# Conditional MLP on one core: TensorE's loop at a fixed slot, seven short warm-ups, first weights rounded in halves, and EPS added on GpSimd

## The chip, the cores and the metric

The kernel runs on 1 core of one Trainium2 chip. The metric is the device time of one execution in microseconds (us), the median over several runs.

## What is computed

Sixteen sequences of 512 tokens with 512 features go through one of three small MLPs. Which one is known only at run time, from an integer for each sequence:

```python
out_nr  = gelu(x @ w1_nr  + b1_nr)  @ w2_nr  + b2_nr
out_tsr = gelu(x @ w1_tsr + b1_tsr) @ w2_tsr + b2_tsr
h       = gelu(x @ w1_sr  + b1_sr)            # 512 -> 1024
out_sr  = gelu(h @ w2_sr + b2_sr) @ w3_sr + b3_sr
y = x + where(c == 0, out_nr, where(c == 1, out_tsr, out_sr))
return (y - mean(y)) * rsqrt(var(y) + 1e-5) * gamma + beta
```

All inputs are float32. The drawn conditions are 0 2 0 0 0 0 0 1 2 2 1 2 0 2 2 1: seven sequences of kind NR (0), three of TSR (1), six of SR (2).

## The kernel before

**Products.** Every float32 factor is split into a part rounded to TensorE's fp32r form (`_hi`) and the rest (`_lo`), and each product of 128x128 by 128x512 is three matmuls: hi·hi, hi·lo, lo·hi (`product`, lines 243 to 246; `part`, line 278, for the first layer of NR). A matmul is a weight load and a matmul instruction. An NR or TSR sequence takes 96 matmuls, an SR sequence 240: 10 x 96 + 6 x 240 = 2400.

**Engines.** One sequence is one batch of the loop. TensorE makes the products in PSUM. ScalarE rounds x to `x_hi`, applies the gelu twice (L415 to `g_hi`, L416 back to the bank) and later scales y by `rstd` (L437). VectorE makes `g_lo` (L467) and `x_lo` (L472), adds the residual (L482), takes statistics (L487, L491), adds EPS to the variance (`variance`, L499), and subtracts the mean (`centre`, L494). GpSimd adds the last bias to the residual rows (L616), takes the power -0.5 (`deviations`, L620), adds beta (L628), and in the first two batches splits the SR and TSR weights into hi and lo (L590, L595, L606). SyncE issues the transfers. Semaphores order all of it; each engine works off its own program strictly in order.

**Order around the change.** ScalarE finishes the four tiles of one batch before it starts the gelus of the next. So the first gelus of batch 1 come after the last `rstd` of batch 0, and with them the first `g_lo` that TensorE needs 48 matmuls into batch 1. GpSimd's program in batch 0 (NR) is: bias of tiles 0 and 1, a half of an SR weight pair, bias of tiles 2 and 3, `deviations(0, 2)`, `split_hi` of the pair sr2 0, `deviations(2, 2)`, `split_lo` of that pair, then the pairs sr1 2, sr1 3, sr2 1 and so on. TensorE needs sr1 3 72 matmuls into batch 1, after its first two hidden products of layer 2.

**The start.** TensorE begins with matmuls on a constant: 9 with 512 columns and then 14 with 128 columns (`N_WARM`, `N_WARM_SHORT`), while x and the first weights are loaded and split. For the first two chunks of `w_hi` VectorE does the rounding itself (L570), and TensorE waits for each on `s_first_w` before its first use.

**Control flow.** TensorE's loop over the 16 batches is written by hand (`kinds`): tests for NR, SR, TSR; each body starts with a branch prefetch hint (L388) for the branch at its end (L390), then the loop's own compare and branch (L406) leads back. The other engines' branches have no hints.

Of the kernel before, what the change touches and what calls it, by code (L numbers as in the profile page):

```python
# [6 lines left out]
NBATCH = 16  # L7
T = 512
H = 512
HC = H // P  # L10
TT = T // P
EPS = 1e-5
# [25 lines left out]
FINISHED_BY_OTHERS_END = TT - 1  # L38

N_WARM, N_WARM_SHORT = 9, 14

def conditional_mlp(nc, x, x_t, cond, weights, bias_cols, rows, out):
    fp32, fp32r, i32 = mybir.dt.float32, mybir.dt.float32r, mybir.dt.int32
    ALU, ACT = mybir.AluOpType, mybir.ActivationFunctionType
    ctx = ExitStack()
    with ctx:  # L48
        def sb(name, shape, dt=fp32):
            return ctx.enter_context(nc.sbuf_tensor(name, shape, dt))  # L50

        def sem(name):
            return ctx.enter_context(nc.semaphore(name))
# [4 lines left out]
        w_raw = nc.alloc_sbuf_tensor_at("w_raw", [P, N_WCHUNK, H], fp32, offset=w_place)  # L58
        w_lo = nc.alloc_sbuf_tensor_at("w_lo", [P, N_WCHUNK, H], fp32r, offset=w_place)
        w_hi = sb("w_hi", [P, N_WCHUNK, H], fp32r)  # L60
# [10 lines left out]
        mv = sb("mv", [P, TT, 2])  # L71
        var_eps = sb("var_eps", [P, TT])
# [27 lines left out]
        s_first, s_first_w, s_nr = sem("s_first"), sem("s_first_w"), sem("s_nr")  # L100
# [3 lines left out]
        s_y, s_acc = sem("s_y"), sem("s_acc")  # L104
        s_row = [sem(f"s_x_row{t}") for t in range(TT)]
        s_xb, s_ev, s_bn, s_mv = sem("s_xb"), sem("s_ev"), sem("s_bn"), sem("s_mv")
        s_var = sem("s_var")
        s_own = sem("s_own")
        s_rstd, s_rstd_end = sem("s_rstd"), sem("s_rstd_end")
        s_v, s_v_end = sem("s_v"), sem("s_v_end")  # L110
# [4 lines left out]
        def take(eng, s, n=1):  # L115
            eng.wait_ge(s, n)
            eng.sem_inc(s, -n)  # L117
# [124 lines left out]
        def _(eng):  # L242
# [18 lines left out]
            def last_layer(w, order, claim):  # L261
                seen = 0
                for j, t in order:
                    if j == seen:
                        take(eng, s_gs)
                        seen += 1
                    if claim and j == 0:
                        take(eng, s_acc)
                    n = bass.ts(t, P)
                    sums = product(bank[4 + t][:, :], g_hi[:, j, n], g_lo[:, j, n], w_hi[:, w + j, :], w_lo[:, w + j, :],  # L270
                                   j == 0, j == HC - 1)
                    if j == HC - 1:
                        sums.then_inc(s_y, 1)

            def x_taken(f):

                eng.sem_inc(s_stage[f], 1)

            def part(j, c, which):

                dst, n, w = bank[j][:, :], bass.ts(j, P), W1[NR] + c
                a, b = (w_lo if which == 2 else w_hi), (x_lo if which == 1 else x_hi)
                return eng.matmul(dst, a[:, w, n], b[:, c, :], start=c == 0 and which == 0, stop=c == HC - 1 and which == 2)

            def step(kind, read_next):
                if kind == NR:
                    take(eng, s_x01, 1)
                    for c in range(2):
                        eng.wait_ge(s_first, c + 1)
                        eng.wait_ge(s_first_w, c + 1)  # L290
                        for which in range(3):
                            if which == 1:
                                if c == 0:
                                    eng.wait_ge(s_nr, 1)
                                else:
                                    take(eng, s_x01, 1)
                                    x_taken(0)
                            if which == 2:
                                eng.wait_ge(s_nr, 2 + c)
                            for j in range(HC):  # L300
                                part(j, c, which)
                        if c == 0:
                            read_next()
                    take(eng, s_x23, 1)
                    for c in (2, 3):
                        if c == 3:
                            take(eng, s_x23, 1)
                            x_taken(1)
                        eng.wait_ge(s_first, 3 + c)
                        if c == 2:  # L310
                            eng.wait_ge(s_nr, 4)
                        for j in range(2):
                            part(j, c, 0)
                            part(j, c, 1)
                        eng.wait_ge(s_nr, 3 + c)
                        for j in range(2):
                            sums = part(j, c, 2)
                            if c == 3:
                                sums.then_inc(s_h, 1)
                    for j in (2, 3):  # L320
                        for c in (2, 3):
                            for which in range(3):
                                sums = part(j, c, which)
                        sums.then_inc(s_h, 1)
                    eng.wait_ge(s_nr, 8)
                    last_layer(W2[kind], ORDER, claim=True)
                    return
                take(eng, s_x01, 2)
                x_taken(0)
                take(eng, s_x23, 2)  # L330
                x_taken(1)
                if kind == NONE:
                    read_next()
                    return
                if kind == TSR:
                    eng.wait_ge(s_split["tsr"], 4)
                    for j in range(HC):
                        layer1(kind, j)
                        if j == 0:
                            read_next()  # L340
                    last_layer(W2[kind], ORDER, claim=True)
                    return
                for j in range(4):
                    if j >= 2:
                        take(eng, s_acc)
                    layer1(kind, j)
                    if j == 0:
                        read_next()
                for first in (0, 2, 4):
                    eng.wait_ge(s_split["sr2"], first // 2 + 1)  # L350
                    for j in (first, first + 1):
                        if j != 1:
                            take(eng, s_gs)
                        for i in range(HC):
                            if j == 0 and i == 2:
                                take(eng, s_gs)
                            layer2_sr(j, i)
                    if first < 4:
                        for j in (first + 4, first + 5):
                            if j < 6:  # L360
                                take(eng, s_acc)
                            eng.wait_ge(s_split["sr1"], 4)
                            layer1(kind, j)
                eng.wait_ge(s_split["sr2"], 4)
                take(eng, s_gs, 2)
                for i in range(HC):
                    layer2_sr(6, i)
                    layer2_sr(7, i).then_inc(s_h, 1)
                eng.wait_ge(s_split["sr3"], 2)
                last_layer(W3[SR], ORDER_SR, claim=False)  # L370
# [32 lines left out]
                body(NONE)  # L403
                nc.switch_bb("tensor_kinds_end")

            with eng.Fori(0, NBATCH) as b:  # L406
                kinds(b)

        @block.scalar
# [54 lines left out]
        def _(eng):  # L464
# [24 lines left out]
            def moments(kind, t):  # L489
                take(eng, s_bn)  # L490
                eng.bn_aggr(mv[:, t, :], bn[:, t, :]).then_inc(s_mv, 1)  # L491
# [5 lines left out]
            def variance(t, n=1):  # L497
                take(eng, s_mv, n)
                eng.tensor_scalar(var_eps[:, t:t + n], mv[:, t:t + n, 1], EPS, None, ALU.add).then_inc(s_var, n)  # L499
# [15 lines left out]
            def body(kind, read_next):  # L515
                read_next()
                hidden(kind)
                split_x(0, s_x01, 2)
                split_x(1, s_x23, 2)
                eng.wait_ge(s_rows, 16)  # L520
                for t in range(0, TT, 2):
                    residual(kind, t)
                    residual(kind, t + 1)
                    stats(kind, t)
                    stats(kind, t + 1)
                    moments(kind, t)
                    moments(kind, t + 1)
                    variance(t, 2)
                    centre(kind, t)
                    centre(kind, t + 1)  # L530

# [35 lines left out]

            for c in range(2):
                eng.wait_ge(s_w_piece[c], 16)
                eng.tensor_copy(w_hi[:, c, :], w_raw[:, c, :]).then_inc(s_first_w, 1)  # L570
                x_low(c, c + 1, (s_nr, s_x01)[c])
                eng.wait_ge(s_first_w, c + 1)
                w_low(c, 0)
            x_low(2, 3, s_nr)
            x_low(3, 4, s_x23)
# [10 lines left out]
        def _(eng):  # L586
# [29 lines left out]
                        eng.tensor_tensor(y[:, t, :], y[:, t, :], row[:, kind, :], ALU.add).then_inc(s_xb, 1)  # L616

            def deviations(t, n):
                take(eng, s_var, n)
                eng.tensor_tensor(rstd[:, t:t + n], var_eps[:, t:t + n], power[:, t:t + n], ALU.pow).then_inc(s_rstd, n)  # L620

            def deviation_end(t, done=s_rstd):
# [149 lines left out]
```

## Time and profile before

| | us |
|---|---|
| three runs | 559.85, 559.77, 558.93 (median 559.77) |
| the profiled execution | 559.41 |
| its span, first to last instruction | 557.7 |
| outside the span | 1.7 |

| engine | busy us | share of the span |
|---|---|---|
| TensorE, matmuls (PE) | 549.6 | 99% |
| TensorE, weight loads (PEld) | 453.4 | 81% |
| VectorE (DVE) | 273.9 | 49% |
| GpSimd (POOL) | 248.3 | 45% |
| ScalarE (ACT) | 213.5 | 38% |

Times in the rows are counted from the start of the span. A matmul's duration of 389 ns is longer than its pace, because consecutive matmuls overlap; the pace is the distance between two starts. A name with a q (DVEq) is an engine's sequencer, which waits, branches and issues.

### The profile page before, as it was taken

How to read it: one execution, taken by the hardware profiler on the slowest of the kernel's cores; microseconds unless marked ns; L12 is line 12 of the kernel's file. 1: busy time of each engine (PE TensorE's matmuls, PEld its weight loads, DVE VectorE, ACT ScalarE, POOL GpSimd, SP SyncE). 2: the span in 40 equal slices, each digit the busy share in tenths (PEclk: the TensorE clock that was granted, in tenths of full speed). 3: DMA queues.
4: the chain of work that ended last, by engine and by line, in shares of the span. 5: the costliest groups of instructions: out<-in, count | busy, mean ns of one | idle time of the engine just before them, and what ended most of it. 6: DMA issues, size and time to landing. Idle time of an engine off the chain costs nothing. (4 is left out here: it accounts for less than half of the span.)

```text
span 557.7 us, 8222 instructions
## 1 busy us (share of the span) xinstructions
PE 549.6 (99%) x2423; PEld 453.4 (81%) x2424; DVE 273.9 (49%) x448; ACT 213.5 (38%) x328; POOL 248.3 (45%) x196
## 2 busy tenths in 40 slices
PE   9999999999999999999999999999999999999994
PEld 6888888888888888888888888888888888888883
DVE  5660176775856956114710569112765105601657
ACT  5451336145244354214421452424255124513351
POOL 0979898765674575300430046600174300430056
PEclk9999999999999999999999999999999999999998
DMA  8876405245344444200320044400244100410032
GB/s 313 339 237 190 152 7 196 100 151 188 109 155 145 156 150 141 84 0 0 138 87 0 1 158 142 150 0 0 75 150 159 66 0 29 154 43 0 0 135 91
DMA packets 26370, 61.28 MB, mean 110 GB/s; under 512 B 3058, under 2 KB 3314, under 8 KB 26226
## 3 DMA queue, kind: packets, MB, share of 16 engines
q1 hardware_dynamic: 26208, 60.97, 31.9%
q8 instruction: 6, 0.10, 0.1%
q10 hardware_dynamic: 146, 0.13, 0.1%
q14 instruction: 10, 0.08, 0.1%
HBM read 44.31 MB, written 16.78 MB: 110 GB/s over the span
## 5 line engine op out<-in xcount | busy, mean ns | idle before, releaser
L467 DVE TENSOR_TENSOR g_lo<-bank,g_hi 128x512 fp32r<-128x512 f32 x112 | 77.5, 692 | 251.0 <-DVEq L117 250.9
L415 ACT ACTIVATE g_hi<-bank,bcol 128x512 fp32r<-128x512 f32 x112 | 77.9, 695 | 165.9 <-ACTq L117 164.7
L620 POOL TENSOR_TENSOR rstd<-var_eps,power 128x2 f32<-128x2 f32 x30 | 21.0, 699 | 239.7 <-POOLq L117 239.7
L616 POOL TENSOR_TENSOR y<-y,row 128x512 f32<-128x512 f32 x64 | 95.7, 1514 | 49.1 <-POOLq L117 48.9
L437 ACT ACTIVATE y<-y,rstd 128x512 f32<-128x512 f32 x63 | 42.3, 717 | 166.3 <-ACTq L117 166.3
L244 PE MATMUL bank<-w_hi,g_hi 128*128 128x512 f32 x256 | 99.6, 389 | 0.0
L245 PE MATMUL bank<-w_lo,g_hi 128*128 128x512 f32 x256 | 99.6, 389 | 0.0
L246 PE MATMUL bank<-w_hi,g_lo 128*128 128x512 f32 x256 | 99.6, 389 | 0.0
L244 PE MATMUL bank<-x_hi,w_hi 128*128 128x512 f32 x240 | 93.4, 389 | 0.0
L245 PE MATMUL bank<-x_lo,w_hi 128*128 128x512 f32 x240 | 93.4, 389 | 0.0
L246 PE MATMUL bank<-x_hi,w_lo 128*128 128x512 f32 x240 | 93.4, 389 | 0.0
L628 POOL TENSOR_TENSOR y<-y,row 128x512 f32<-128x512 f32 x63 | 79.5, 1296 | 0.0
L244 PE MATMUL bank<-g_hi,w_hi 128*128 128x512 f32 x192 | 74.7, 389 | 0.0
L245 PE MATMUL bank<-g_lo,w_hi 128*128 128x512 f32 x192 | 74.7, 389 | 0.0
L246 PE MATMUL bank<-g_hi,w_lo 128*128 128x512 f32 x192 | 74.7, 389 | 0.0
L416 ACT ACTIVATE bank<-bank,bcol 128x512 f32<-128x512 f32 x112 | 74.3, 664 | 0.0
L244 PEld LDWEIGHTS bank<-w_hi,g_hi 128*128 128x128 f32 x256 | 48.1, 188 | 10.0
L245 PEld LDWEIGHTS bank<-w_lo,g_hi 128*128 128x128 f32 x256 | 48.1, 188 | 10.0
L246 PEld LDWEIGHTS bank<-w_hi,g_lo 128*128 128x128 f32 x256 | 48.1, 188 | 9.9
L472 DVE TENSOR_TENSOR x_lo<-stage,x_hi 128x1024 fp32r<-128x1024 f32 x30 | 51.6, 1757 | 4.3 <-DVEq L117 4.3
L245 PEld LDWEIGHTS bank<-x_lo,w_hi 128*128 128x128 f32 x240 | 45.1, 188 | 9.3
L246 PEld LDWEIGHTS bank<-x_hi,w_lo 128*128 128x128 f32 x240 | 45.1, 188 | 9.3
(42 smaller groups left out, 580.2 us busy)
## 6 DMA issues: line engine op xcount, KB each, us to landing
y<-x SPq DMA_DIRECT2D x64, 256.0 KB, 3.6
out<-y SPq DMA_DIRECT2D x63, 256.0 KB, 2.5
stage<-x_t SPq DMA_DIRECT2D x31, 512.0 KB, 3.3
w_raw<-weights SPq DMA_DIRECT2D x17, 512.0 KB, 5.1
row<-rows SPq DMA_DIRECT2D x1, 1280.0 KB, 11.0
stage<-x_t SPq DMA_DIRECT2D x2, 256.0 KB, 3.2
w_raw<-weights SPq DMA_DIRECT2D x2, 256.0 KB, 4.0
out<-y SPq DMA_DIRECT2D x1, 128.0 KB, 1.9
```

The costliest lines, as they stand in the source:

```text
L244: eng.matmul(dst, a_hi, b_hi, start=first, stop=False)
L245: eng.matmul(dst, a_hi, b_lo, start=False, stop=False)
L246: return eng.matmul(dst, a_lo, b_hi, start=False, stop=final)
L415: eng.activation(g_hi[:, slot, :], psum, ACT.Gelu, bias=b)
L416: eng.activation(psum, psum, ACT.Gelu, bias=b).then_inc(s_g, 1)
L437: eng.activation(y[:, t, :], y[:, t, :], ACT.Copy, scale=rstd[:, t:t + 1]).then_inc(s_n, 1)
L467: eng.tensor_tensor(g_lo[:, slot, :], psum, g_hi32[:, slot, :], ALU.subtract).then_inc(s_gs, 1)
L472: eng.tensor_tensor(x_lo[:, c, :], stage[:, f, :, :], x_hi32[:, c, :], ALU.subtract).then_inc(done, n)
L616: eng.tensor_tensor(y[:, t, :], y[:, t, :], row[:, kind, :], ALU.add).then_inc(s_xb, 1)
L620: eng.tensor_tensor(rstd[:, t:t + n], var_eps[:, t:t + n], power[:, t:t + n], ALU.pow).then_inc(s_rstd, n)
L628: eng.tensor_tensor(y[:, t, :], y[:, t, :], row[:, R_BETA, :], ALU.add).then_inc(s_fin, 1)
```

## The change

The first two weight chunks are rounded in halves of 256 columns, each half with its own increment of `s_first_w`, and TensorE waits for a half where it first uses it (output chunks 0 and 2 of `which == 0`). For tiles 0 and 1 of every batch but the last, VectorE no longer adds EPS: it only passes a semaphore on, and GpSimd adds EPS itself before the power. Tiles 2 and 3 stay as they were.

```diff
-N_WARM, N_WARM_SHORT = 9, 14
+N_WARM, N_WARM_SHORT = 9, 7
+
+LOOP_SLOT = 80
...
-        s_var = sem("s_var")
+        s_moments, s_eps, s_var = sem("s_moments"), sem("s_eps"), sem("s_var")
...
                     for c in range(2):
                         eng.wait_ge(s_first, c + 1)
-                        eng.wait_ge(s_first_w, c + 1)
                         for which in range(3):
...
                             for j in range(HC):
+                                if which == 0 and j % 2 == 0:
+                                    eng.wait_ge(s_first_w, 2 * c + j // 2 + 1)
                                 part(j, c, which)
...
-            with eng.Fori(0, NBATCH) as b:
+
+            with nc.Fori(0, NBATCH, engines=[eng.engine], head_slot={eng.engine: LOOP_SLOT}) as b:
                 kinds(b)
...
                     moments(kind, t + 1)
-                    variance(t, 2)
+                    if t == 0:
+                        take(eng, s_mv, 2)
+                        eng.sem_inc(s_moments, 2)
+                    else:
+                        variance(t, 2)
                     centre(kind, t)
...
                 eng.wait_ge(s_w_piece[c], 16)
-                eng.tensor_copy(w_hi[:, c, :], w_raw[:, c, :]).then_inc(s_first_w, 1)
+                for half in (slice(0, H // 2), slice(H // 2, H)):
+                    eng.tensor_copy(w_hi[:, c, half], w_raw[:, c, half]).then_inc(s_first_w, 1)
                 x_low(c, c + 1, (s_nr, s_x01)[c])
-                eng.wait_ge(s_first_w, c + 1)
+                eng.wait_ge(s_first_w, 2 * c + 2)
                 w_low(c, 0)
...
             def deviations(t, n):
-                take(eng, s_var, n)
+
+                if t == 0:
+                    take(eng, s_moments, n)
+                    eng.tensor_scalar(var_eps[:, t:t + n], mv[:, t:t + n, 1], EPS, None, ALU.add).then_inc(s_eps, n)
+                    take(eng, s_eps, n)
+                else:
+                    take(eng, s_var, n)
                 eng.tensor_tensor(rstd[:, t:t + n], var_eps[:, t:t + n], power[:, t:t + n], ALU.pow).then_inc(s_rstd, n)
```

## Rows read from the trace of the kernel before

**Rows 1.** The page: busy time by engine, busy tenths of TensorE, granted clock.
```profile
PE 549.6 (99%) x2423; PEld 453.4 (81%) x2424; DVE 273.9 (49%) x448; ACT 213.5 (38%) x328; POOL 248.3 (45%) x196
...
PEclk9999999999999999999999999999999999999998
```
**Rows 2.** Timeline, TensorE, ends of the stream: start, length, engine, line, tiles, count.
```profile
4.61 1.70 PE L375 MATMUL bank<-const-bfloat16-1.0 128*128 128x128 bf16 x14
6.07 1.24 PE L283 MATMUL bank<-x_hi,w_hi 128*128 128x512 f32 x4
7.15 1.07 PE L283 MATMUL bank<-x_lo,w_hi 128*128 128x512 f32 x4
...
550.01 0.39 PE L246 MATMUL bank<-w_hi,g_lo 128*128 128x512 f32 x1
```
**Rows 3.** Timeline, TensorE's weight loads at the start.
```profile
3.76 0.15 PEld L373 LDWEIGHTS bank<-const-bfloat16-1.0 128*128 128x128 bf16 x1 [0.28 <-issue]
4.18 0.15 PEld L375 LDWEIGHTS bank<-const-bfloat16-1.0 128*128 128x128 bf16 x1 [0.28 <-issue]
...
6.00 0.88 PEld L283 LDWEIGHTS bank<-x_hi,w_hi 128*128 128x128 f32 x4
6.92 0.87 PEld L283 LDWEIGHTS bank<-x_lo,w_hi 128*128 128x128 f32 x4
7.83 0.87 PEld L283 LDWEIGHTS bank<-x_hi,w_lo 128*128 128x128 f32 x4
```
**Rows 4.** Timeline, VectorE and ScalarE at the start.
```profile
3.40 0.62 ACT L444 CAST x_hi<-stage 128x512 fp32r<-128x512 f32 x1 [0.57 <-DMA stage<-x_t]
4.43 0.43 DVE L570 CAST w_hi<-w_raw 128x512 fp32r<-128x512 f32 x1 [3.53 <-DMA w_raw<-weights]
4.78 0.69 DVE L560 TENSOR_TENSOR x_lo<-stage,x_hi 128x512 fp32r<-128x512 f32 x1
5.38 0.68 DVE L560 TENSOR_TENSOR w_lo<-w_raw,w_hi 128x512 fp32r<-128x512 f32 x1
7.05 0.43 DVE L570 CAST w_hi<-w_raw 128x512 fp32r<-128x512 f32 x1 [0.99 <-DMA w_raw<-weights]
```
**Rows 5.** Timeline, VectorE across the end of batch 0.
```profile
27.64 1.14 DVE L499 TENSOR_SCALAR var_eps<-mv 128x2 f32<-128x2 f32 x1
28.70 1.40 DVE L494 SCALAR_TENSOR_TENSOR y<-bank,mv,row 128x512 f32<-128x512 f32 x2
...
32.97 0.17 DVE L499 TENSOR_SCALAR var_eps<-mv 128x2 f32<-128x2 f32 x1
33.05 1.40 DVE L494 SCALAR_TENSOR_TENSOR y<-bank,mv,row 128x512 f32<-128x512 f32 x2
37.65 1.47 DVE L467 TENSOR_TENSOR g_lo<-bank,g_hi 128x512 fp32r<-128x512 f32 x2 [3.20 <-DVEq L117]
```
**Rows 6.** Timeline, GpSimd from the biases of batch 0 to sr1 3.
```profile
26.23 2.53 POOL L616 TENSOR_TENSOR y<-y,row 128x512 f32<-128x512 f32 x2
28.97 0.72 POOL L620 TENSOR_TENSOR rstd<-var_eps,power 128x2 f32<-128x2 f32 x1 [0.21 <-POOLq L117]
29.66 1.06 POOL L590 TENSOR_SCALAR w_hi<-w_raw 128x1024 fp32r<-128x1024 f32 x1
33.33 0.70 POOL L620 TENSOR_TENSOR rstd<-var_eps,power 128x2 f32<-128x2 f32 x1 [2.60 <-POOLq L117]
...
41.20 2.40 POOL L595 TENSOR_TENSOR w_lo<-w_raw,w_hi 128x1024 fp32r<-128x1024 f32 x1 [0.18 <-POOLq L117]
```
**Rows 7.** Timeline, ScalarE from the tiles of batch 0 to batch 1's gelu.
```profile
29.80 1.34 ACT L437 ACTIVATE y<-y,rstd 128x512 f32<-128x512 f32 x2 [8.25 <-ACTq L117]
34.15 1.34 ACT L437 ACTIVATE y<-y,rstd 128x512 f32<-128x512 f32 x2 [3.01 <-ACTq L117]
35.88 0.69 ACT L415 ACTIVATE g_hi<-bank,bcol 128x512 fp32r<-128x512 f32 x1 [0.40 <-ACTq L117]
```
**Rows 8.** Timeline, weight loads of batch 1: its first, g_lo's first, sr1 3's first.
```profile
27.78 0.19 PEld L244 LDWEIGHTS bank<-x_hi,w_hi 128*128 128x128 f32 x1
...
38.66 0.19 PEld L244 LDWEIGHTS bank<-g_hi,w_hi 128*128 128x128 f32 x1
...
44.10 0.19 PEld L244 LDWEIGHTS bank<-x_hi,w_hi 128*128 128x128 f32 x1
```
**Rows 9.** By line: L499 on VectorE and GpSimd's smallest operations.
```profile
L499 DVE TENSOR_SCALAR var_eps<-mv x34: 136/169/1142, 27.6 to 553.1; 128x2 f32<-128x2 f32 x30, 128x1 f32<-128x1 f32 x4
...
0.78 0.10 POOL L645 MEMSET power<- 128x4 f32 x1 [0.29 <-POOLq L766]
```
**Rows 10.** TensorE's sequencer, L406 and the hint L388, whole span and around 25 us.
```profile
L406 PEldq COMPARE_BRANCH  x16: 76/213/252, 24.6 to 546.5; - x16
...
L388 PEldq BRANCH_PREFETCH_HINT  x1: 46/46/46, 25.6 to 25.6; - x1
```
**Rows 11.** The page, DMA queues: packets, MB, share. Queues that carry instructions.
```profile
q8 instruction: 6, 0.10, 0.1%
...
q14 instruction: 10, 0.08, 0.1%
```
**Rows 12.** Timeline, VectorE at the end of the span.
```profile
550.40 0.74 DVE L494 SCALAR_TENSOR_TENSOR y<-bank,mv,row 128x512 f32<-128x512 f32 x1
551.05 0.69 DVE L482 TENSOR_TENSOR bank<-bank,y 128x512 f32<-128x512 f32 x1
...
554.32 0.88 DVE L505 SCALAR_TENSOR_TENSOR y<-y,rstd,row 128x256 f32<-128x256 f32 x2 [0.44 <-DVEq L117]
```

## The prediction

> **What bounds the kernel now.** I read the page first: matmuls are busy 99% of the span, every other engine at most half [rows 1]. Then I looked whether TensorE ever pauses. The first real matmul starts at 6.07 us and the last at 550.01 [rows 2]; between them lie 2399 steps, so the mean pace is (550.01 - 6.07)/2399 = 0.2267 us. The stretch from 7.15 to 7.83 in the weight loads, and those around 38.66 and 44.10, have that same pace [rows 3, 8]: (44.10 - 38.66)/24 = 0.2267, (38.66 - 27.78)/48 = 0.2267. A mean over the whole run that equals the pace of single stretches leaves no room for stalls: all of them together are under about 0.2 us. So the time is a sum of three parts: 6.07 before the stream, 543.9 of stream, and 557.7 - 550.01 = 7.7 of tail; with 1.7 outside the span this is the profiled 559.41. The change removes no matmul of the stream, so it can only move the start, move the tail, or put a stall into a stream that has none.
>
> What sets 6.07? The last short warm-up. x_hi is rounded at 3.40 + 0.62 = 4.02 and w_hi at 4.43 + 0.43 = 4.86 [rows 4], while the 14 short warm-ups start at 4.61 and follow one another up to 6.07 [rows 2]. TensorE's real work is ready 1.1 us before it begins.
>
> **Warm-ups, 14 to 7.** The clock first. The 14 warm-ups of 128 columns fill 4.61 to about 6.1, (6.07 - 4.61)/14 = 0.104 us or slightly more each, and the long ones are 0.42 apart (3.76, 4.18) [rows 2, 3]: 512 columns at 1.2 GHz. The four first real weight loads start at 6.00 to 6.69 and the next four at 6.92, i.e. 0.92 for four against 0.91 (7.83 - 6.92) for the next [rows 3]; the matmuls take 7.15 - 6.07 = 1.08 for four, one at 0.39 and three at 0.23. So the level rises to 2.4 GHz inside the first real matmul, after 5.4 us of unbroken work; the page's clock line, which begins with that rise, shows full clock from there to the end of the stream [rows 1]. Seven warm-ups fewer let the first real matmul start 7 x 0.107 = 0.75 us earlier, at 5.32 (0.107 = 0.427/4, a quarter of the columns). If the clock still rises near 6.2, the 0.9 us from 5.32 to 6.2 run at 0.427 per matmul: 2.1 matmuls done, where before 0.3 to 0.4 were. That is 1.75 matmuls ahead, 1.75 x 0.227 = **0.40 us** gained. The other 0.35 us of the 0.75 are lost to the slow clock. Had the clock risen before the short warm-ups, they would cost about half each, and the gain is again 7 x 0.054 = 0.38.
>
> **What the stream then meets.** TensorE arrives 0.40 earlier everywhere; what doesn't follow it can become late. In the first chunk: x_lo ends at 5.47 and is needed at 6.92 - 0.40, w_lo ends at 6.06 and is needed at 7.83 - 0.40 [rows 3, 4]. The second w_hi is bound by its transfer and ends at 7.48; its first use comes four matmuls after the last row of rows 3 (7.83 + 0.91 = 8.74), less 0.40 = 8.34. All have 0.85 or more.
>
> **Halves.** Two rounding operations of 0.43 become four of about half. No row shows a 256-column rounding; bounds for the addition are 0 and the whole of a smallest VectorE operation, 0.17 [rows 9], once per chunk. I take 0.06. It delays x_lo and w_lo by that, inside covers of 0.85; the first half is ready some 0.2 earlier, but 4.86 is already before 5.32. Price and gain: **0**. It would matter only if the clock rises before the short warm-ups, when the first use comes near 5.0 and the second chunk's near 7.6.
>
> **EPS.** The place to look is the end of batch 0. VectorE's L499 takes 0.17 as a rule but 1.14 at 27.64 [rows 5, 9], and it ends at 28.78, when GpSimd's two bias additions end (26.23 + 2.53 = 28.76) [rows 6]: it sat behind them. The next one takes VectorE only 0.08 (32.97 to 33.05) [rows 5]. What follows hangs on it: `centre` at 28.70, the second L499 at 32.97, GpSimd's power at 33.33 after an idle 2.60, ScalarE's tiles at 34.15, its first gelu of batch 1 at 35.88, g_lo at 37.65 [rows 5 to 7]. g_lo's first half-pair ends at 37.65 + 0.69 = 38.34, and TensorE takes it at 38.66 [rows 8]: 0.32 of cover, of which the handover takes some. Likewise sr1 3: w_lo ends at 41.20 + 2.40 = 43.60, needed at 44.10: 0.50 [rows 6, 8]. Neither follows TensorE's start, since VectorE in this stretch waits for GpSimd's biases, and those for transfers. So an earlier start alone would use up these 0.32, and gain 0.0 to 0.3 instead of 0.40.
>
> With the edit VectorE passes the semaphore at about 27.6 and goes to `centre`, 1.14 - 0.08 = **1.06 us earlier**. The residual of tiles 2 and 3 needs biases that end at 27.5 and 28.76, so it can follow. GpSimd adds EPS from about 28.95: price between 0.10 (its memset) and 0.72 (its power) [rows 6, 9], plus 0.18 for taking its own semaphore (the idle time before L595, rows 6). I take 0.25 + 0.18, since a 2-column addition is nearer to the memset. The power then ends at about 30.1 (29.9 to 30.6), split_hi of 1.06 at 31.2 (at most 31.7), before the second power can start at 33.33 - 1.06 = 32.3. ScalarE's first two tiles start at 30.2 to 30.8 and take 1.34, done by 32.1, before 34.15 - 1.06 = 33.1. So both chains arrive 1.0 earlier, g_lo at about 37.3 and sr1 3 at 42.6, against needs of 38.26 and 43.70. Cover: 1.0 and 1.1. In later batches the first `rstd` comes 0.3 to 0.8 later and `centre` 0.1 earlier; queued behind GpSimd's new operation are only its second power, which waits for VectorE anyway, and the beta additions. The power waited for VectorE by 2.6 us in batch 0, and 33.33 - 28.97 = 4.4 us lie between the two powers. I take 0 for this; above, 0.1.
>
> **The loop's place.** TensorE's loop branch costs its sequencer 0.21 (0.25 at most), and it is at the next body's hint at 25.6 while the weight loads of that body start at 27.78 [rows 8, 10]: 2.2 us ahead. Queue 8 moved 6 packets of instructions in the whole run, 16 KB each [rows 11]; 16 passes over three kinds cannot be refetched with so few, so the loop stays loaded. Where no fetch costs anything, a better place has nothing to give: **0**. Its first entry gains one taken branch, 0.2 us, at about 3 to 4 us, more than 1 us before 5.32. Below zero it cannot go, as no stall is there to be removed.
>
> The Trainium skill, "Runtime: NRT & Kernel Launch", section on instruction fetch mechanics, says that a taken branch whose target lies outside the window that is loaded has to wait for a fetch. VectorE's idle 3.20 before 37.65 [rows 5] is such a case as far as the rows go, TensorE's rows show none; by that rule a worse place would be the second rival below.
>
> **The tail.** No edit touches the last batch. VectorE works without a break from TensorE's last matmuls to 554.32 + 0.88 [rows 12], so the tail moves with the stream: 0.
>
> **Sum.** -0.40 (warm-ups) + 0 + 0 + 0 + 0 = -0.40 against the profiled 559.41: 559.0. The profiled execution is 0.36 under the median of the three runs; the median of all four is 559.6, and I predict **559.2**, which is that less 0.40. Runs differ by 0.9 us already. The Trainium skill ("TensorE: Matmul & The Clock Gate", the HAM clock gate) says that the moment of the rise varies from run to run because its window runs free; this trace has one rise and doesn't show it. If it holds, runs with an early rise were held up before at 38.66 and are freed by the EPS edit, up to about 0.7 more.
>
> **The rivals.**
> 1. The earlier start is given back: something else in batch 0 or 1 that is tied to a transfer is late (g_lo or a weight pair), because VectorE's sequencer spends its 3.20 us whenever it gets there, or more at another place in its code. For it: the cover was 0.32 and VectorE's code grows. Against: 1.06 us come free. Time: 559.6. Chance 0.15.
> 2. Slower: the new place puts a piece of TensorE's loop where its hint doesn't cover it. Price of one miss: VectorE's 3.20 less the lead of 2.2 = 1.0 us; in the first passes over each kind one to three of them, 560.2 to 562.2; if every pass misses, 16 us. It decides if the loop spills into one more block than before. Against it: 6 packets only, and the hints. 561. Chance 0.08.
> 3. Slower: with less work ahead of it the clock rises later. If it took its 5.4 us anew from 5.32, it would rise at 10.7 and cost half of 4.5 us: 561.5. Against: the real matmuls follow without a gap and keep TensorE as busy. Chance 0.04.
> 4. Early rises are common and the freed 38.66 counts: 558.3 to 558.6. Chance 0.12.
>
> Forecast 0.61 (558.8 to 559.5).
>
> **Range and chances.** 558.2 to 560.0 takes in the forecast, rivals 1 and 4, and the spread of the runs. About 0.2%, or 1.1 us, is what a measurement of this kernel can tell from no change. Faster by more than that: part of rival 4, 0.06. Slower: rivals 2 and 3 mostly, 0.09. Within: 0.85.
>
> **What the profile will show.** The first L283 matmul at about 5.3 and the last L246 near 549.6; first four real matmuls over a longer time than 1.08; L494 of batch 0 at 27.6 in place of 28.70, and g_lo near 36.6 in place of 37.65; a GpSimd operation of 0.1 to 0.7 ahead of each first power; still 2400 matmuls at 0.2267. A pause in TensorE's loads near a batch's beginning would prove rival 2, one near 38.3 or 43.7 rival 1.

## The result and the profile after

The changed kernel takes 560.81 us (median of 13 runs, 560.28 to 561.29) against 559.77 for the kernel before (13 runs): ratio 1.0019, 95% interval 1.0012 to 1.0027. It is **1.0 us slower**, where 0.4 us faster was forecast. The profiled execution took 560.53 us, its span is 558.5 against 557.7.

First the page, in the lines that answer to [rows 1] and [rows 11], and TensorE's waits (engine, line, waited for: us, times, longest).

```profile
PE 549.4 (98%) x2416; PEld 452.2 (81%) x2417; DVE 271.9 (49%) x435; ACT 213.5 (38%) x328; POOL 251.8 (45%) x211
...
PEclk9999999999999999999999999999999999999998
...
q8 instruction: 7, 0.11, 0.1%
...
PE bank L246 <- PEq L119: 1.0, 1, 1.0
```

The kernel before has no wait of a real matmul in this view; now there is one, of 1.0 us, and it is put down to TensorE's own sequencer. Queue 8 carries one packet of instructions more. Next the timeline of TensorE, matmuls and then weight loads, which answers to [rows 2] and [rows 8]; bracketed is the idle time ahead of a row.

```profile
4.62 0.93 PE L378 MATMUL bank<-const-bfloat16-1.0 128*128 128x128 bf16 x7
5.33 1.20 PE L285 MATMUL bank<-x_hi,w_hi 128*128 128x512 f32 x4
6.37 1.07 PE L285 MATMUL bank<-x_lo,w_hi 128*128 128x512 f32 x4
7.28 1.07 PE L285 MATMUL bank<-x_hi,w_lo 128*128 128x512 f32 x4
8.26 1.16 PE L285 MATMUL bank<-x_hi,w_hi 128*128 128x512 f32 x4
...
11.15 0.42 PE L285 MATMUL bank<-x_hi,w_hi 128*128 128x512 f32 x1
...
27.34 0.39 PE L248 MATMUL bank<-w_hi,g_lo 128*128 128x512 f32 x1
28.75 0.47 PE L246 MATMUL bank<-x_hi,w_hi 128*128 128x512 f32 x1 [1.02 <-PEq L119]
...
550.87 0.39 PE L248 MATMUL bank<-w_hi,g_lo 128*128 128x512 f32 x1
```
```profile
27.12 0.19 PEld L248 LDWEIGHTS bank<-w_hi,g_lo 128*128 128x128 f32 x1
28.72 0.19 PEld L246 LDWEIGHTS bank<-x_hi,w_hi 128*128 128x128 f32 x1 [1.41 <-issue]
```

Between the last matmul of batch 0 (27.34) and the first of batch 1 (28.75) lie 1.41 us where the pace is 0.227. What the sequencer did there stands in the view of the line of the branch that ends a body (L393 after, L390 before; durations in ns: least, median, most): first after, over the whole span, then before.

```profile
L393 PEldq COMPARE_BRANCH  x16: 184/184/3365, 23.5 to 547.0; - x16
```
```profile
L390 PEldq COMPARE_BRANCH  x16: 184/194/449, 23.9 to 546.2; - x16
```

One of the 16 branches, the first, takes 3365 ns in place of 449. It is the one at the end of the first NR body, which starts at 23.51 and ends at 26.88. The trace has a 16 KB packet of instructions on queue 8 that starts at 24.38, after the branch's start. In the kernel before that packet starts at 21.34, ahead of the branch at 23.94.

The sum of the change, from the starts of matmuls (rows above and [rows 2, 8]):

| stretch | before | after | difference |
|---|---|---|---|
| span's start to first real matmul | 6.07 | 5.33 | -0.74 |
| that one to the 25th (before: 11.68) | 5.61 | 5.82 | +0.21 |
| 25th to batch 1's first (28.00, 28.75) | 16.32 | 17.60 | +1.28 |
| batch 1's first to the last (550.01, 550.87) | 522.01 | 522.12 | +0.11 |
| last matmul's start to the end | 7.7 | 7.7 | 0 |
| sum | 557.7 | 558.5 | +0.86 |

### The profile page after: what moved, and what is told of

Its sections match the earlier page's. It is cut to its first block and busy times, and to the rows that moved or that the text cites. A ratio compares the mean times of both kernels' runs of the same rounds, so it can differ in the third digit from the quotient of the medians.

```text
span 558.5 us, 8241 instructions
## 1 busy us (share of the span) xinstructions
PE 549.4 (98%) x2416; PEld 452.2 (81%) x2417; DVE 271.9 (49%) x435; ACT 213.5 (38%) x328; POOL 251.8 (45%) x211
## 5 line engine op out<-in xcount | busy, mean ns | idle before, releaser
L631 POOL TENSOR_SCALAR var_eps<-mv 128x2 f32<-128x2 f32 x15 | 3.3, 217 | 185.6 <-POOLq L119 185.4
L246 PEld LDWEIGHTS bank<-x_hi,w_hi 128*128 128x128 f32 x240 | 45.0, 188 | 10.7 <-issue 1.4
```

Source lines behind the costliest of these rows:

```text
L246: eng.matmul(dst, a_hi, b_hi, start=first, stop=False)
```

## The experiments

All times are medians; the kernel before, run beside them, took 559.6 to 559.9. The letters of the theories are those of the expectations. The measured branch is the one at the end of the first NR body, the pause is what TensorE loses at the start of batch 1 over its pace. Branch and pause come from one profiled execution of each kernel; whether they repeat in the other executions is not shown.

### Which part costs

**The change with a plain loop.** Edit against the changed kernel:
```diff
-            with nc.Fori(0, NBATCH, engines=[eng.engine], head_slot={eng.engine: LOOP_SLOT}) as b:
+            with eng.Fori(0, NBATCH) as b:
```

> The changed kernel with a plain loop, so that its head lies wherever the 7 fewer warm-ups leave it. Theory A (the fixed place makes the loop branch at the end of the first NR body wait for its code: 3.37 us on TensorE's sequencer against 0.45 before): the branch takes 0.45 or less, no pause near 28.7 us, time 559.0 to 559.5. Theory B (the sequencer, with fewer warm-ups queued, issues its hint at 3.3 in place of 4.4 us, and the hint is lost): the 3.4 us branch and the 1.2 us pause stay, 560.8. Theory C (any place other than the old one has a miss): the branch is long too, 560.8, but then not by the time of the hint.

Measured 560.59, ratio 1.0017 (1.0008 to 1.0027); branch 3726 ns, pause 1.6 us. So A falls: without the slot the branch is as long.

**The slot alone**, put into the kernel before (head_slot 80 in its loop).

> The kernel before with the head of TensorE's loop at slot 80 and nothing else. A: the branch at the end of the first NR body takes 3 us or more, one pause of about 1.2 us near 28 us, time 561.0 against 559.8 of before. B: no pause, 559.8. C: as A, if slot 80 is not where the loop lay before.

560.71, ratio 1.0017 (1.0007 to 1.0026); but the branch took 2291 ns and the pause was only 0.13 us. The profiled execution lost more elsewhere: 0.9 at the third chunk, where ScalarE's w_hi was late, and 0.5 where batch 1 first takes g_lo and the pair sr1 3. The slot costs here, and little of it at the branch.

**The warm-ups alone** (`N_WARM_SHORT` 7).

> The kernel before with 7 short warm-ups, nothing else; the loop's head moves 14 instructions forward. A: no long branch; the start is 0.75 us earlier, but the g_lo that TensorE takes at 38.66 ends at 38.3 whatever TensorE does, so the gain is 0.0 to 0.3 us: 559.5 to 559.8. B: a branch of 3.4 us at the end of the first NR body, pause 1.2 us, 560.6 to 561.

559.47, ratio 0.9995 (0.9985 to 1.0005): no change that can be told. Branch 2349 ns, pause 0.2 us.

**EPS alone** (the hunks of `variance` and `deviations`).

> The kernel before with EPS of tiles 0 and 1 added on GpSimd, nothing else; TensorE's program is that of before. All theories: within 0.3 us of before (559.5 to 559.8); the first g_lo of batch 1 ends about 1 us earlier than 38.34, and TensorE has 1.0 to 1.4 us of cover there in place of 0.32. If the EPS edit is itself the cost, 560.5 or more.

559.33, ratio 0.9991 (0.9981 to 1.0000). Branch 449 ns. VectorE's timeline at the end of batch 0 in this kernel, which answers to [rows 5]:

```profile
28.64 0.41 DVE L491 BATCH_NORM_AGGREGATE mv<-bn 128x2 f32<-128x6 f32 x2
29.30 1.41 DVE L494 SCALAR_TENSOR_TENSOR y<-bank,mv,row 128x512 f32<-128x512 f32 x2 [0.25 <-DVEq L117]
...
33.58 0.17 DVE L499 TENSOR_SCALAR var_eps<-mv 128x2 f32<-128x2 f32 x1
```

From the start of the aggregates to `centre` it is 0.66 us; before, where the aggregates start at 27.09, it was 28.70 - 27.09 = 1.61 [rows 5]. The edit frees 0.95 us there. This execution needed them: its loads landed later than those of [rows 5], and g_lo still ended at 38.58 (37.88 + 0.69), just ahead of the weight load at 38.65 that takes it.

**The halves alone**, in the kernel before:
```diff
-                        eng.wait_ge(s_first_w, c + 1)
...
+                                if which == 0 and j % 2 == 0:
+                                    eng.wait_ge(s_first_w, 2 * c + j // 2 + 1)
...
-                eng.tensor_copy(w_hi[:, c, :], w_raw[:, c, :]).then_inc(s_first_w, 1)
+                for half in (slice(0, H // 2), slice(H // 2, H)):
+                    eng.tensor_copy(w_hi[:, c, half], w_raw[:, c, half]).then_inc(s_first_w, 1)
...
```

> The kernel before with the first weights rounded in halves, nothing else; the loop's place stays. A: branch 0.45 us, 559.7 plus or minus 0.3. Halves as the cause: branch 2 us or more and 560.5 or more.

560.73, ratio 1.0021 (1.0012 to 1.0030); branch 3666 ns, pause 1.6 us. The halves alone bring a loss as large as the change's, without adding an instruction to TensorE's program: its loads only carry other waits.

**Warm-ups and EPS, without halves and slot.**

> 7 warm-ups and the EPS edit, no fixed slot, no halves. If the halves make the difference between the 560.6 of the changed kernel without its slot and the 559.5 of the warm-ups alone: branch about 2.3 us, pause 0.1 to 0.2 us, 559.0 to 559.5. If the EPS edit together with the early start does: branch 3.3 to 3.7 us, 560.5. If it is the chance of the profiled execution (the same place, so the same fetch): branch anywhere between 2.3 and 3.7.

559.31, ratio 0.9993 (0.9984 to 1.0003); branch 2409 ns, pause 0.27. This half of the change does what was forecast, as near as it can be measured: 0.35 us below the kernel before, in an interval that holds zero.

**The same with slot 80.**

> 7 warm-ups, the EPS edit and the fixed slot 80, without the halves: the change but for its third part. If slot and halves each cost what they cost alone (0.98 and 1.07) because each makes the same branch wait, this one still has a long branch of 2.3 to 3.6 us and takes 559.4 to 560.8; with the 2.3 us of the slot alone, pause under 0.3 us at 28 us and 559.5. If the slot alone costs by another way (late loads at the start, an extra fetch), 560.3 or more.

560.46, ratio 1.0013 (1.0004 to 1.0022): the slot costs 1.15 us here (560.46 against 559.31), and with it no halves are needed for a loss. The two costs do not add up. In the changed kernel, where the halves are in, the slot costs 0.2 (560.81 against the 560.59 of the plain loop); and where the slot is in, the halves cost 0.35 (560.81 against 560.46). Leaving out one of them would not have saved the change. Branch 2656 ns, pause 0.55; and TensorE waited 0.7 us for the second w_hi:

```profile
PE bank L285 <- DVE w_hi L577: 0.7, 1, 0.7
PE bank L246 <- PEq L119: 0.3, 1, 0.3
```

### Is it the loop's place?

**Slots 94, 110 and 66** in the changed kernel.

> The changed kernel with its loop head at slot 94 in place of 80. Theory A (the head of the kernel before lies at about slot 94, and 7 fewer warm-ups bring it to about 80; what counts is how far ahead of the branch at the end of the first NR body TensorE enters its next block of instructions, since that is when the code behind the branch is fetched; slot 94 puts the crossing 14 instructions earlier than slot 80): the branch takes 0.45 us, its fetch starts near 21 us and not behind the branch, no pause near 28 us, time 559.0 to 559.4. Theory D (it is the wait in front of the branch, or the moved start, and not the place): branch 2 to 3.7 us, time 560.5 or more.

> The changed kernel with slot 110. A: the block is entered 30 instructions (3.4 us) earlier than with slot 80, branch 0.2 to 0.45 us, no pause near 28 us, 559.0 to 559.4; but the end of the loop spills over one more block boundary, which may cost at another branch, in the first passes. D: as slot 80, 560.5 or more.

> The changed kernel with slot 66. A: the block is entered 14 instructions later than with slot 80, 24 instructions ahead of the branch; the branch takes the whole fetch, 3.3 to 3.8 us, pause 1.2 to 1.6 us at about 28.7, time 560.5 to 561.3. If the place doesn't matter: like slot 94.

560.73 (1.0009 to 1.0027), 560.67 (1.0007 to 1.0026) and, in a single execution, 560.38. Branches 3396, 3604 and 2977 ns. No slot cures it. Slot 110 alone has no packet of instructions at 5 to 6 us (slots 66, 80 and 94 have), which I read so (no run shows where the blocks end): its head still fits into the block of the code ahead of it, the others' are pushed into the next, and the head of the changed kernel's plain loop lies between 94 and 110.

**The old place, kept by 14 semaphore updates** ahead of a plain loop.
```diff
+            for n in range(14):
+                eng.sem_inc(s_fill, 1 if n % 2 == 0 else -1)
             eng.sem_inc(s_acc, 4)
...
```

> The changed kernel without the fixed slot, and with 14 semaphore updates of TensorE's sequencer in the place of the 14 instructions of the 7 warm-ups that went. The loop has the place and its head the time (about 4.2 us) that it has in the kernel before; start, halves and EPS edit are those of the change. Theory A (place): branch at the end of the first NR body 0.45 us, its fetch near 21 us, no pause near 28 us, 559.0 to 559.4. Theory E (halves or the early arrival cause the miss, wherever the loop lies): branch 2.3 to 3.7 us, 560.5 or more.

560.76, ratio 1.0020 (1.0011 to 1.0029); branch 3546 ns. And the same without the halves:

> 7 warm-ups and the EPS edit, no halves, no slot, and 14 semaphore updates of TensorE's sequencer that keep the loop where the kernel before has it. Theory A' (without the halves the place decides between a branch of 0.45 and one of 2.3 us): branch 0.45 us, fetch near 21 us, no pause at 28 us, 558.9 to 559.3, faster than the kernel before and about 0.2 us faster than without the 14 updates. Otherwise as without them: 559.3, branch 2.4 us.

560.30, ratio 1.0013 (1.0004 to 1.0022), branch 3469 ns, pause 1.3. That one fell on the wrong side of every theory: no halves, the old place, the hint at the old time, and a long branch. Without the 14 updates the same kernel took 559.31. So the old place does not bring the short branch back.

**No hints**, in the kernel before.

> The kernel before without its branch hints (and so with one instruction fewer in each body). If the fetch at 21.3 us that serves the branch at the end of the first NR body comes from the hint: this fetch is gone, the branch takes 3 us or more, and TensorE pauses 1.2 us near 28 us: 561. If it comes from going on into the next block: branch 0.45 us as before, no pause there.

A single execution: 561.92; branch 5319 ns, no packet ahead of it, pause 3.0 us. TensorE's weight loads:

```profile
26.90 0.19 PEld L246 LDWEIGHTS bank<-w_hi,g_lo 128*128 128x128 f32 x1
30.19 0.19 PEld L244 LDWEIGHTS bank<-x_hi,w_hi 128*128 128x128 f32 x1 [3.10 <-issue]
```

The hints are most likely what makes the 449 ns, though this edit also takes an instruction out of each body. The changed kernel's 3.4 us lie between the branch before and the one without hints.

### Is it the halves' wait, VectorE, or the moment?

**One more wait, long fulfilled, on the third weight load.**
```diff
+                                if which == 0 and j == 2:
+                                    eng.wait_ge(s_first_w, c + 1)
```

> The kernel before with one thing more: in the first chunk products of NR, TensorE's third weight load of each chunk waits for s_first_w once more, which is long reached. No instruction is added, two weight loads only carry a wait. Theory F (what makes the fetch behind the hint come too late in the version with halves is the wait on TensorE's own weight load): branch 3.3 to 3.7 us, 560.5 to 560.9. Theory G (it is the way VectorE now works, or the timing of the start): branch 0.45 us, 559.7.

559.69, ratio 0.9999 (0.9990 to 1.0009), branch 449 ns. F falls.

**Halves on VectorE, one wait on TensorE** (`s_first_w` at `2 * c + 2`, in the old place).

> The kernel before with w_hi rounded in halves on VectorE, but TensorE waiting once for both halves, in the place of its old wait. F: branch 0.45 us, 559.7 plus or minus 0.3. G: branch 2 us or more, 560.5 or more.

559.80, ratio 1.0002 (0.9993 to 1.0011), branch 449 ns. G falls too, as far as it blames VectorE.

**The moment, moved with nothing else.** 256 columns in the short warm-ups of the kernel with halves, 32 in those of the kernel before.

> The kernel before with the first weights in halves, and with its 14 short warm-ups of 256 columns in place of 128: same instructions, same places, but TensorE's real work begins 0.7 to 1.5 us later than with halves alone. Theory T (what decides is when TensorE's sequencer comes to the last waits of the first NR body: in all runs without a slot so far, at 21.15 us or later the branch took 0.45, at 20.9 it took 2.4, at 20.65 or earlier 3.5 to 3.7): it comes there after 21.1 us, branch 0.45 us, no pause of a microsecond at batch 1, 559.8 to 560.4 in spite of the later start. Theory H (the halves with an early wait cause it, whenever): branch 3.5 us, 561 or more.

> The kernel before with its 14 short warm-ups of 32 columns in place of 128: same instructions, same places, no halves, no EPS edit, but TensorE's real work can begin up to 1.0 us earlier. T: the last waits of the first NR body are reached before 21.0 us, the branch takes 2.3 to 3.7 us, and the time is 559.5 to 560.7. Place theory (the loop's place decides): branch 0.45 us, 559.2 to 559.7.

The late one: 561.10, ratio 1.0030 (1.0020 to 1.0039), branch 3506 ns although it started at 24.3 us. The early one: 559.72, ratio 1.0002 (0.9993 to 1.0012), branch 449 ns although it started at 23.6. T falls: both are on the wrong side (the last waits came at 21.6 in the late one, at 20.8 in the early one). The early one shows something else. VectorE and TensorE's weight loads around its first g_lo of batch 1:

```profile
38.06 0.69 DVE L467 TENSOR_TENSOR g_lo<-bank,g_hi 128x512 fp32r<-128x512 f32 x1 [2.87 <-DVEq L117]
```
```profile
38.04 0.19 PEld L246 LDWEIGHTS bank<-x_hi,w_lo 128*128 128x128 f32 x1
38.82 0.19 PEld L244 LDWEIGHTS bank<-g_hi,w_hi 128*128 128x128 f32 x1 [0.60 <-issue]
```

g_lo ends at 38.75 and the load that takes it starts at 38.82, 0.45 late. TensorE began 0.9 us earlier here (5.14) and gave it back, partly to the slow clock and partly at this place.

**The hint nearer to its branch**, in the change with a plain loop: marked ahead of each body's last layer.
```diff
                     eng.wait_ge(s_nr, 8)
+                    hint()
                     last_layer(W2[kind], ORDER, claim=True)
...
```

> The changed kernel without its slot, and with each hint moved from the top of its body to the front of the body's last layer (in NR 105 instructions and some 9 us ahead of the branch in place of 212 instructions and 20 us). Theory L (the hint at the top of the first body is not acted upon in the kernels with the long branch, by whatever it is lost on the way): the nearer hint is acted upon, branch 0.45 us, no pause at 28 us, 559.0 to 559.4, so faster than the kernel before. Theory S (the fetch is asked for in time and stands behind the loads): the branch stays at 2.3 to 3.7 us and the time at 560.6.

560.68, ratio 1.0016 (1.0007 to 1.0025). The branch shrank from 3726 to 2461 ns and the pause from 1.6 to 0.2 us, but not the median. The profiled execution waited 1.4 us for the first w_hi instead, whose transfer came late (its rounding started at 6.17, where it was 4.43 before). Neither L nor S is borne out whole.

### What the branches have in common

| first branch, ns | pause, us | kernels |
|---|---|---|
| 449 | none | before; EPS; one more wait; halves with one wait; early warm-ups |
| 2291 to 2656 | 0.13 to 0.55 | slot alone; warm-ups; warm-ups + EPS, with and without slot 80; near hint |
| 2977 to 3726 | 0.9 to 1.6 | the change, with any slot or none; halves; halves late; both kept in place by 14 updates |
| 5319 | 3.0 | no hints |

The pause is the branch's time less 2.1 to 2.4 us in every kernel that has one. And the branch waits for its packet: in all 14 kernels of the second and third class it ends 2.49 to 2.60 us after the start of one 16 KB packet on queue 8. So what makes it long is when that packet starts, and within a class this lies near one distance from the branch: 2.4 to 2.6 us ahead of it in the first class; between 0.24 ahead and 0.15 behind in the second; 0.9 to 1.2 behind it in the third (0.4 with slot 66). The late halves moved branch and packet together, by about 1 us each, over the halves alone. That speaks against a fetch that only queues behind the loads, but does not prove it.

What puts a kernel into its class stays open. One more wait, VectorE's halves with one wait, EPS and an earlier arrival left the branch at 449 ns. The slot alone and the warm-ups alone brought 2.3 us, the halves with their earlier waits 3.7, and 14 updates that restore the place 3.5. No single one of place, waits and moment of arrival orders these rows. Nor does the clock: its level rose between 3.5 and 6.8 us in the third class and between 5.3 and 6.6 in the first. The kernel before took 559.6 to 559.9 on six chips. The variants ran on one chip each, so whether a variant keeps its class on another is not tested.

## Why the prediction was wrong, point by point

**What bounds the kernel.** Right: the stream still runs at 0.2267 per matmul, and the time is start, stream, stalls and tail.

**Warm-ups, -0.40.** The start moved by 0.74 (0.75 forecast). The clock's level rose at 5.39 in this execution and at 6.23 in the one before, both times inside the first real matmul (1.04 for the first four, 1.08 before), so the slow clock took nothing of the 0.74, where I had given it 0.35. That is luck of this execution: in the 20 profiled ones the rise lies anywhere from 3.50 to 6.75. With it moves the start: where the 14 warm-ups of 128 columns are kept and w_hi is there in time, the first real matmul lies between 5.25 and 6.07. The start of the stream took about 0.2 back (second row of the table): for example, the four matmuls from 7.28 to 8.26 took 0.98 in place of 0.91, where the second w_hi's rounding began at 7.82 in place of 7.05. I had put that cover at 0.85 from one execution; the landings vary by as much. Over ten runs warm-ups and EPS together gave 0.35, in an interval that holds zero.

**Halves, 0.** The step that failed. I priced the two roundings on VectorE and looked for what is late in data. Alone they cost 1.07 us, and not through VectorE's work: in the profiled execution a branch of TensorE's sequencer took 3.67 us in place of 0.45 and brought 1.6 us of pause. In the two kernels that part them, their cost comes only together with the earlier waits. Why such a wait should delay a fetch some 15 us later stays open.

**EPS, 0 with 1.06 us freed.** Right in what it frees: 0.95, GpSimd's addition 0.22 (0.25 taken) and 0.18 for its own semaphore. The rows of GpSimd after, answering to [rows 6]:

```profile
29.67 0.22 POOL L631 TENSOR_SCALAR var_eps<-mv 128x2 f32<-128x2 f32 x1
30.07 0.72 POOL L635 TENSOR_TENSOR rstd<-var_eps,power 128x2 f32<-128x2 f32 x1 [0.18 <-POOLq L119]
```

VectorE's rows of the same stretch, after:

```profile
27.92 0.41 DVE L495 BATCH_NORM_AGGREGATE mv<-bn 128x2 f32<-128x6 f32 x2
28.58 1.41 DVE L498 SCALAR_TENSOR_TENSOR y<-bank,mv,row 128x512 f32<-128x512 f32 x2 [0.25 <-DVEq L119]
...
37.17 0.69 DVE L471 TENSOR_TENSOR g_lo<-bank,g_hi 128x512 fp32r<-128x512 f32 x1 [2.82 <-DVEq L119]
```

The aggregates began 0.83 later than before (27.92, 27.09), so `centre` came only 0.12 earlier and g_lo at 37.17, not at the 27.6 and 36.6 that I had named as signs. The prediction had held these moments fixed because they hang on transfers; they move with them from execution to execution. Nothing was lost by it, as TensorE came later still.

That an earlier start alone runs into this g_lo is shown by the early warm-ups above, though it ended at 38.75 there and not at 38.3.

**The loop's place, 0.** The second step that failed. "Where no fetch costs anything, a better place has nothing to give" holds; but the premise was false. I took the absence of stalls and the few packets as evidence that no fetch costs anything and a new place is harmless, and I read the loop's own branch (L406, 0.25 at most), not the first passage of L390, which took 449 ns before as well, against 194 as a rule. In the first pass the code behind the branch still has to be fetched, and the sequencer's lead of 2.2 us covers such a fetch only in part: after, the branch took 3.37 us, and TensorE lost 1.3. The slot costs 1.0 to 1.15 us in two pairs of kernels, and 0.2 in the third, where the halves are in. In the traces part of it is lost at the branch (0.13 and 0.55) and more while the first weights come (0.9 each). That the additional packet of instructions among those loads delays them is only argued: the landings vary by as much without a slot.

**Rival 2** had the mechanism (a branch that waits for its code, once, on the first pass; price 3.2 less 2.2 = 1.0 each) at a chance of 0.08. The measured one costs 3.37 less 2.1 = 1.3. What it had wrong is the cause: it is not the slot's alone. Its sign, a pause in TensorE's loads near a batch's beginning, came (28.72 after 27.12), but it does not prove the slot guilty: the halves alone, in the old loop, show the same pause. The rule that I set beside it is in the Trainium skill, "Runtime: NRT & Kernel Launch", instruction fetch mechanics: a taken branch outside the loaded window waits for a fetch. The traces agree with it, by the 5319 ns without hints and by this kernel's later branches at 184 to 413, once the code is there. **Rival 1** (a late g_lo or weight pair) did not occur in the change. **Rival 3** (a later clock) is out: the clock rose no later. **Rival 4** (early rises freed by EPS): early rises are common, but EPS alone gave 0.4 us, in an interval that reaches zero.

**Range.** 558.2 to 560.0 missed 560.81. It was made of the runs' spread and the data's covers; rival 2, the one that came nearest to what happened, was left outside at 561.

## What to carry to other kernels

TensorE's program in front of a matmul stream has two supplies to watch, the data and the code. Where a large loop body ended in a branch to code not yet fetched, its sequencer had about 2.1 us in hand here, and a fetch that came late cost up to 1.6 us, without hints 3. So every edit ahead of the first such branch, even one that only moves a wait, should be followed by a look at that branch's duration. Try the parts of a bundle one by one: here two of four were harmless, and each of the other two, alone, cost more than the whole bundle could gain.

## What the runs showed that I had not expected

- TensorE's first branch at the end of a body took 0.45 us where its packet of instructions started 2.4 us or more ahead of it, 2.3 to 3.7 where the packet came with the branch or after it, and 5.3 without hints; later passes take 0.18 to 0.9.
- Two TensorE programs that differ only in the values that three waits ask for (one more wait, and the halves) took 0.45 and 3.67 us at a branch some 15 us later. VectorE's programs differ too, by the halves.
- The first rounding of w_hi started between 4.4 and 6.2 us in the 20 profiled executions of these kernels, though its transfer was issued at the same time (about 1.2 us). The start of this kernel is uncertain by more than the 0.75 us of the warm-ups that were taken out.
